# A graph network kernel: GpSimd waits for its gathers to land after every eight

## What is computed

```python
h = relu(layernorm(x))
# layer 0: edge MLP, maximum over the edges of a node
e = concat([h[dst], h[src] - h[dst]]) ; m = relu(e @ W1 + b1) @ W2 + b2
x = x + segment_max(m, dst)
h = relu(layernorm(x))
# layer 1: edge MLP with batch norm, sum over the edges, node MLP with batch norm
o = concat([h[src], edge_attr]) ; o = relu(bn(o @ W1a + b1a)) @ W2a + b2a
s = segment_sum(o, dst)
x = x + relu(bn(concat([h, s]) @ W1b + b1b)) @ W2b + b2b
```

## Time and profile before

| | |
|---|---|
| median of three runs | 6153.37 us |
| the profiled execution, its own time | 6172.69 us |
| its span, first to last instruction | 6170.9 us |
| busy: PE / PEld / DVE / ACT / POOL | 40% / 24% / 33% / 23% / 58% |
| granted TensorE clock, mean | 0.656 |
| GB/s over the span | 113 |

### The profile page before, as it was taken

One profiled execution on the slowest core, in us unless ns is written; L12 is line 12 of the kernel. 1 busy time (PEld: TensorE's weight loads), 2 busy tenths in 40 slices (PEclk: granted clock), 3 DMA queues, 4 the chain that ended last, 5 costly groups with the idle time before them and its releaser, 6 DMA issues. The chain is left out here.

```text
span 6170.9 us, 34418 instructions
## 1 busy us (share of the span) xinstructions
PE 2478.8 (40%) x8675; PEld 1481.8 (24%) x8675; DVE 2036.0 (33%) x2739; ACT 1424.0 (23%) x2694; POOL 3574.8 (58%) x3776
## 2 busy tenths in 40 slices
PE   2024443333434434333033333433443333347777
PEld 1012222222222222222012121212221211125555
DVE  5212222222222222222522222222222222249995
ACT  6001111111111111111111121211111111138884
POOL 5666666665666666665666666666666666631112
PEclk9975655665665565665556666666666666668887
DMA  9412222222222222222223333333323323249993
GB/s 359 139 48 62 67 67 63 62 66 62 65 65 68 63 67 63 65 62 60 51 74 95 92 93 89 92 86 95 94 84 95 94 84 95 83 150 420 423 421 136
DMA packets 351136, 696.89 MB, mean 113 GB/s; under 512 B 133446, under 2 KB 190544, under 8 KB 304248
## 3 DMA queue, kind: packets, MB, share of 16 engines
q1 hardware_dynamic: 204908, 558.27, 24.7%
q0 software_dynamic: 119328, 128.91, 10.5%
q10 hardware_dynamic: 26706, 7.50, 0.6%
HBM read 349.70 MB, written 344.74 MB: 113 GB/s over the span
## 5 line engine op out<-in xcount | busy, mean ns | idle before, releaser
L715 POOL DMA_INDIRECT send_in<-send_table,send_idx x1664 | 1574.0, 946 | 979.5 <-issue 492.9
L1000 POOL DMA_INDIRECT pairs<-norm_table,send_idx x1664 | 1573.8, 946 | 856.2 <-issue 488.7
L727 PE MATMUL ps_msg<-hidden,w_twice 128*128 128x512 f32 x416 | 416.9, 1104 | 1530.1 <-ACT hidden L780 1069.2
L1021 PE MATMUL ps_hid<-pairs_t,w1a 128*128 128x512 f32 x832 | 623.4, 841 | 1004.6 <-issue 737.1
L1117 DVE TENSOR_SCALAR hid<-ps_hid,vec 128x512 f32<-128x512 f32 x416 | 310.5, 746 | 1814.2 <-DMA recv_edges<-hid,start_idx 1041.2
L1056 ACT COPY pairs_t<-ps_pairs 128x512 f32<-128x512 f32 x416 | 244.0, 587 | 1550.2 <-DMA recv_edges<-node_sums 1048.2
L1014 PE MATMUL ps_pairs<-ident,pairs 128*128 128x128 f32 x1664 | 352.1, 351 | 481.3 <-issue 261.4
L805 DVE TENSOR_TENSOR_SCAN filled<-mask,filled,ps_recv 128x512 f32<-128x512 f32 x208 | 266.2, 1280 | 826.2 <-issue 470.4
L1250 DVE TENSOR_TENSOR_SCAN total<-ps_mask,total,hid 128x1024 f32<-128x1024 f32 x208 | 488.7, 2350 | 50.6 <-PE ps_mask L1200 24.7
L796 DVE TENSOR_TENSOR_SCAN maxima<-mask,maxima,ps_msg 128x512 f32<-128x512 f32 x208 | 266.1, 1279 | 678.1 <-PE ps_msg L727 336.9
L727 PEld LDWEIGHTS ps_msg<-hidden,w_twice 128*128 128x128 f32 x416 | 97.5, 291 | 1591.0 <-ACT hidden L780 1109.2
(11 more groups left out here) (176 smaller groups left out, 3045.1 us busy)
## 6 DMA issues: line engine op xcount, KB each, us to landing
hid_edges<-hid SPq DMA_DIRECT2D x104, 1024.0 KB
hid<-hid_edges SPq DMA_DIRECT2D x104, 1024.0 KB
hid_edges<-rows SPq DMA_DIRECT2D x104, 1024.0 KB
recv_edges<-node_sums SPq DMA_DIRECT2D x52, 1024.0 KB
recv_in<-recv_edges SPq DMA_DIRECT2D x208, 256.0 KB
max_edges<-max_rows SPq DMA_DIRECT2D x208, 256.0 KB
edge_in<-in_edge_attr_dram SPq DMA_DIRECT2D x415, 128.0 KB
send_in<-send_table,send_idx POOLq DMA_INDIRECT x1664
```

The source lines that it names most:

```text
L715: pool.indirect_dma_start(out=send_in[:, s, j, t, :], out_offset=None, in_=send_table, in_offset=bass.IndirectOffsetOnAxis(ap=send_idx[:, ...
L727: nc.tensor.matmul(ps_msg[:, :], w2_twice[:, :], hidden[:, s % 2, :], start=True, stop=True).then_inc(msg_done, 1)
L1000: pool.indirect_dma_start(out=pairs[:, s, j, 0:C], out_offset=None, in_=norm_table, in_offset=bass.IndirectOffsetOnAxis(ap=send_idx[:, s / ...
L1021: nc.tensor.matmul(ps_hid[s % 2][:, :], w1a[:, :], pairs_t[:, s % 2, :], start=True, stop=True).then_inc(multiplied, 1)
```

## The change

In both gather functions of GpSimd a wait is added behind the waits that stood there. In the first gather stage, before each block but the first, GpSimd waits until the semaphore of the block before has all its steps: 16 for each of eight transfers, in each round. In the second gather stage it does so before every second block (of four transfers each), for the block before that. Nothing else is changed, and the order of the instructions on every engine is as it was.

```diff
                     at_least_apart(pool, send_turned, k - U + 1, pool_passed)
+                    if k > 0:
+                        at_least(pool, gathered[(s - 1) % U], 16 * 2 * J * ((k - 1) // U + 1))
                     for t in range(2):
                         for j in range(J):
...
                     at_least_apart(pool, turned, k - U + 1, pool_passed)
+                    if k % 2 == 0 and k > 0:
+                        at_least(pool, gathered[(s - 1) % U], 16 * J * ((k - 1) // U + 1))
                     for j in range(J):
```

## The result

The changed kernel takes 6201.60 us in the median of four runs (6195.66 to 6205.08), the kernel before beside it 6149.82 us (6135.12 to 6164.97): a ratio of 1.0083, 95% interval 1.0056 to 1.0110. The forecast was 5925 us. The profiled execution has a span of 6193.9 us, 23.0 more than before.

What follows compares the result with a forecast made beforehand. GpSimd's queue was taken to bound both gather stages: 216 and 54 us less idle time, 42 back, made 228 us less than the profiled 6172.7, so 5945, or 5925 us in the median; range 5850 to 6400.

Steps and rivals of the forecast that it cites:

- The bound and the mechanism: Both gather stages: GpSimd's queue sets the pace; TensorE's signals come late during unbroken gather issue, on time after a stop.
- Do the waits for indices go?: GpSimd's 485.3 and 364.5 us of waits for ScalarE's index copies nearly vanish; a twentieth, 42 us, left in.
- the 3.80 us stop: Second gather stage: GpSimd stopped longer than any planned pause, yet ScalarE's copy came 6 us after restart; evidence for stop-too-short.
- Price of one pause: GpSimd's 207 stops per stage: 1.53 us each in the first, 1.65 in the second; 317 and 342 us.
- The bounds: Pause per stop in both stages between 1.53 us (295 us less in all) and 2.83 us (241 us more).
- Dear landing: Rival: landing costs more in the running gather stages, pause 2.83 us with old waits gone; 6395 us, chance 0.10.
- Stop too short: Rival: stops clear nothing, index waits stay and pauses add; 6554 us if all stay, chance 0.22.
- No difference: Rival: each group of eight gathers needs what it needs today, the long wait merely cut up; 6153 us, chance 0.08.
- Issuing early and waiting late: Skill's rule for transfers, cited against the change: following it would give the stop-too-short rival's result.

Runs made afterwards that it cites:

- older_landing: Changed kernel with as many waits at the same places, but for gathers issued 8 to 16 earlier, already landed: 6200.01 us, 1.0024 of before.
- wait_first: Changed kernel with the added waits ahead of those for indices and buffer instead of behind them: 6064.15 us, 0.9800 of before.
- wait_first_again: Kernel of wait_first run again on a third chip, one with late signals: 6058.84 us, 0.9797 of before.
- after_again: The changed kernel, unaltered, run again on the third chip, one with late signals: 6248.78 us, 1.0101 of before.
- stage1_only: Kernel before plus only the added wait of the first gather stage: 6180.08 us, 1.0019 of before.
- idle_short: Kernel before plus a GpSimd fill of an unread 128x768 tile after every eight gathers, no landing wait: 6119.97 us, 0.9923 of before.
- idle_four: Kernel before plus a GpSimd fill of an unread 128x768 tile after every four gathers, no landing wait: 5951.37 us, 0.9650 of before.
- idle_only: Kernel before plus a GpSimd fill of an unread 128x1536 tile after every eight gathers, no landing wait: 5956.72 us, 0.9627 of before.
- idle_mid: Kernel before plus a GpSimd fill of an unread 128x1280 tile after every eight gathers, on the chip without late signals: 5744.19 us, 1.0816 of before.
- after: The changed kernel itself in its first measurement, against the kernel before: 6201.60 us, 1.0083 of before.
- after_third: The changed kernel, unaltered, run once more on the chip without late signals: 6162.72 us, 1.1605 of before.
- stage2_only: Kernel before plus only the added wait of the second gather stage: 6275.04 us, 1.0183 of before.

## Why the prediction was wrong

**The bound and the mechanism** were right for the chip of the first profile. GpSimd's queue paces both stages, and late TensorE signals make its long waits. With the change every "remote" wait in the gather stages is gone. older_landing shows that a wait already met does nothing, the fills that the waits for indices shrink as the gathers are spaced out without any wait for a landing. What in the changed kernel's stops brings every signal on time is not settled: the fills did not.

**"Do the waits for indices go?"** Right, and more fully than forecast: 42 us were left in, nothing stayed. The row that spoke against it, the 3.80 us stop of the earlier trace rows with a signal still late behind it, has nothing like it in the new kernel, whose chain is never late.

**"Price of one pause", the step that failed.** Forecast were 317 and 342 us of pauses. Measured were 471 and 452, and 62 us of extra gaps that were not in the sum: 985 against 659, 326 us more. Less 42 us of leftovers, 10 of plain gaps and 22 in the issues and outside the stretches, this is the whole way from -228 to +23. The landing was read rightly (1.53 in the earlier trace rows; 1.52 and 1.51 in the median here, where I had put 1.65 for the second stage); what I took it for was wrong. I let GpSimd go on at the moment at which TensorE, waiting for the same transfer, starts. GpSimd's first gather starts 0.70 us after that in the first stage and 0.65 in the second, 279 us over 414 stops. An error of this size decides the case: between 5925 and 6153 us lie 0.55 us for each of the 414 stops. wait_first and wait_first_again show that most of it is the place of the wait: ahead of the others the restart is 0.21 and 0.17 us on both chips, and the extra gaps are gone; that the first stage's stops are hardly shorter for it comes from a later landing. That the restart is dearer because the wait is an instruction of its own behind another is my reading; what is shown is that the order alone changes it.

**The bounds** held: a pause of 2.2 lies between 1.53 and 2.83, and the result lies in the range. But all three rows behind it were times of *other* waiting engines: TensorE in the earlier trace rows, VectorE in the earlier trace rows, SyncE's store in the earlier trace rows. None showed GpSimd waiting for its own gather, and the choice between them by traffic did not touch that. The first two were taken as near when they price the landing alone, without the restart.

**The rivals.** "Dear landing" (6395 us, 0.10) is nearest in kind, with half of its price and another place: restart, not landing. (Landings later than forecast were seen all the same, 1.79 and 1.86 us in the first stage of after_again and stage1_only.) "Stop too short" is false for stops of 2.2 us, while for breaks of 0.91 after eight it describes what happened (idle_short, 510 us of waits left), and for breaks of 1.34 and 1.55 us in part. "No difference" asked for late signals that follow the mean rate of gathers. The runs say that the waits for the indices do (idle_four against idle_only), but at the changed kernel's 1.49 us for a gather there is nothing left to follow. The time came close to this rival's by another road.

**Issuing early and waiting late.** To issue a transfer early and wait for it late, as the fixed cost then overlaps (the Trainium skill, "DMA: Bandwidth & Descriptors", Rules for kernel authors), is borne out in full on the chip without late signals: each stop exposes the landing and the restart, 16% in all. On the other chips the stops cost about the same (471 and 452 us in the first result, 476 and 450 on the chip without late signals), but something else pays most of it back.

**What the profile could not tell:** that the 831 us of waits on which every gain rests belong to the chip it was taken on.

## What to carry to other kernels

A wait for a transfer costs the engine its landing *and* its own restart: take the price from a row of the same engine waiting, not of its neighbour, and multiply before trusting a tenth of a microsecond. If the aim is only to give other engines room, a plain fill of 1.4 us after every eight gathers, or of 0.76 us after every four, in place of the landing wait was worth 3.7 and 3.5% (idle_only 5957, idle_four 5951 us, the fastest of this study on that chip), and the wait put ahead of the others 2.0%, where the changed kernel lost 0.8 to 1.0% beside its own kernel before. But compare on more than one chip before keeping any of them: on the chip without late signals fills with breaks of 1.34 to 1.87 us slowed the kernel by 8 to 12%, and the unchanged kernel was the fastest of all.

## What the runs showed of the hardware

- TensorE's semaphore steps reach waiting engines late while GpSimd issues indirect transfers every 1.25 us: 23.5 us in the earlier trace rows, up to 18.1 us over all mask copies. With a fill that spaces the gathers to 1.33, 1.38 and 1.41 us in the mean the longest delay of a mask copy is 15.3, 11.6 and 7.5 us. With a wait for the landing after every eight (1.43 to 1.53 us) none is late. Two of the three chips of the experiments showed this; on the third the same kernel at the same rate (idle_mid) showed none, and the kernel before ran in 5310 instead of 6170 to 6184 us. What differs between the chips is not known.
- GpSimd, waiting for its own transfer, starts its next issue 0.65 to 0.70 us after TensorE, waiting for the same semaphore, has started, in after, after_again, after_third, stage1_only and stage2_only; with the wait ahead of the others 0.17 to 0.21. The landing itself was seen by TensorE 1.51 to 1.86 us after the issue's end in the median, with the wait ahead 2.10 in the first stage and 1.57 to 1.60 in the second.
- In programs with such waits behind others, gaps of 1.86 and 1.67 us stand at fixed gathers (every 96th and every 88th), where nothing is waited for, at the same places on all three chips; with the waits in another order there are none. Their cause was not looked for.
